# First loads, statistics by pairs, product order and bias product in a graph layer on one core

## The reference

```python
def reference(x, adj, W_self, b_self, W_nb, b_nb, W_comb, b_comb):   # x 8192x256 f32, adj 8192x8192 int32
    h = jnp.maximum(_layernorm(x, axis=-1), 0.0)
    mask = (adj > 0).astype(x.dtype)
    deg = jnp.sum(mask, axis=1, keepdims=True)
    agg = mask @ h / jnp.maximum(deg, 1.0)
    combined = jnp.concatenate([h @ W_self + b_self, agg @ W_nb + b_nb], axis=-1)
    return x + jax.nn.relu(combined @ W_comb + b_comb)
```

## Time and profile before

| what | value |
|---|---|
| median of 3 runs | 1001.75 us (1001.56 to 1003.32) |
| profiled execution, its own time | 1001.76 us |
| its span, first to last instruction | 1000.0 us |
| granted TensorE clock, mean | 1.000 |
| busy PE / DVE / ACT / POOL | 989.9 / 673.9 / 585.0 / 30.5 us |
| DMA | 295 GB/s over the span |
| start of main stage (first L360) | 110.50 us |

### The profile page before, as it was taken

One profiled execution on the slowest core, in us unless ns is written; L12 is line 12 of the kernel. 1 busy time (PEld: TensorE's weight loads), 2 busy tenths in 40 slices (PEclk: granted clock), 3 DMA queues, 4 the chain that ended last, 5 costly groups with the idle time before them and its releaser, 6 DMA issues.

```text
span 1000.0 us, 14269 instructions
## 1 busy us (share of the span) xinstructions
PE 989.9 (99%) x4696; PEld 460.5 (46%) x4696; DVE 673.9 (67%) x1163; ACT 585.0 (59%) x675; POOL 30.5 (3%) x73
## 2 busy tenths in 40 slices
PE   7999999999999999999999999999999999999998
PEld 4555444444444444444444444444444444444443
DVE  6886677986776666766667666676666766667711
ACT  5888886775655556655556555565555655556500
POOL 2332000000000000000000000000000000000000
PEclk9999999999999999999999999999999999999999
DMA  9621399999888898888988888888888888888600
GB/s 344 251 85 43 140 421 371 416 420 377 320 316 321 312 341 317 319 322 312 342 312 322 322 313 336 318 322 322 312 328 328 323 315 321 321 326 326 218 16 10
DMA packets 58994, 295.04 MB, mean 295 GB/s; under 512 B 6624, under 2 KB 24160, under 8 KB 26208
## 3 DMA queue, kind: packets, MB, share of 16 engines
q1 hardware_dynamic: 58976, 294.81, 78.6%
HBM read 286.39 MB, written 8.39 MB: 295 GB/s over the span
## 4 chain that ended last, share of the span: by engine, by line
PE 98%; DMA 1%; DVE 0%; SPq 0%; issue 0%
PE pair_ps L360 89%; PE pair_ps L351 8%; PE turn_ps L333 1%; DMA self_f<-in_x_dram 1%; PE pair_ps L381 0%; DVE x_again L439 0%; SPq L195 0%; SPq L193 0%; DVE z L505 0%; DVE fold L502 0%; DVE x_again L442 0%; DVE part L485 0%; DVE part L482 0%; DVE x_again L488 0%; SPq L177 0%
## 5 line engine op out<-in xcount | busy, mean ns | idle before, releaser
L360 PE MATMUL pair_ps<-z,mask_t 128*128 128x512 f16 x4096 | 885.8, 379 | 0.0
L290 ACT ACTIVATE mask<-mask 128x2048 uint8<-128x2048 uint8 x256 | 488.0, 1908 | 341.4 <-DVE mask_t L430 341.4
L360 PEld LDWEIGHTS pair_ps<-z,mask_t 128*128 128x128 fp8e4 x4096 | 396.2, 98 | 475.7
L430 DVE STREAM_TRANSPOSE mask_t<-mask 128x512 uint32<-128x512 uint32 x256 | 181.7, 710 | 219.8 <-PE pair_ps L360 214.3
L424 DVE TENSOR_SCALAR mask<-stage 128x2048 uint8<-128x2048 int32 x256 | 308.1, 1203 | 6.0 <-DMA stage<-in_adj_dram 5.9
L351 PE MATMUL pair_ps<-mask_t 128*128 128x512 f16 x384 | 87.8, 379 | 0.0
L351 PEld LDWEIGHTS pair_ps<-mask_t 128*128 128x128 f16 x384 | 37.6, 98 | 38.6
L290 ACT ACTIVATION_READ_ACCUMULATOR mask<-mask 128x1 f32 x256 | 48.1, 188 | 0.0
L482 DVE SCALAR_TENSOR_TENSOR part<-pair_ps,rdeg,self_f 128x256 f32<-128x256 f32 x64 | 31.0, 484 | 15.7 <-DVE rdeg L477 11.9
L269 ACT ACTIVATE self_f<-self_f,x_again 128x256 f32<-128x256 f32 x64 | 35.0, 605 | 8.7 <-POOL x_again L260 8.7
L447 DVE SCALAR_TENSOR_TENSOR mask_t<-turn_ps,mask_t 128x512 f16<-128x512 f32 x32 | 21.8, 681 | 19.3 <-ACT mask_t L276 19.3
(11 more groups left out here) (31 smaller groups left out, 93.0 us busy)
## 6 DMA issues: line engine op xcount, KB each, us to landing
stage<-in_adj_dram SPq DMA_DIRECT2D x256, 1024.0 KB, 5.9
self_f<-in_x_dram SPq DMA_DIRECT2D x16, 512.0 KB, 15.4
x_again<-in_x_dram SPq DMA_DIRECT2D x64, 128.0 KB, 5.3
out_dram<-x_again SPq DMA_DIRECT2D x64, 128.0 KB, 5.1
z<-in_L_gnn_W_comb_dram SPq DMA_DIRECT2D x2, 256.0 KB, 4.8
z<-in_L_gnn_W_self_dram SPq DMA_DIRECT2D x1, 256.0 KB, 3.6
z<-in_L_gnn_W_nb_dram SPq DMA_DIRECT2D x1, 256.0 KB, 4.5
z<-in_L_gnn_b_comb_dram SPq DMA_DIRECT2D x1, 128.0 KB, 6.4
```

Of the source, the lines that this page charges most:

```text
L290: act.activation(mask[:, a, :], mask[:, a, :], ACT.Copy, accum_out=deg_part[:, n, a:a + 1]).then_inc(counted, 1)
L360: mm = pe.matmul(acc[n], bytes_of[:, :, s], z16[:, SUB * e + s, :], start=(e == 0 and s == 0), stop=(e == CHUNKS - 1 and s == SUB - 1))
L430: dve.transpose(mask_t[:, n, :, a, :], src).then_inc(transposed, 1)
```

## The change

- **Loads.** The weights are packed by the host into two blocks of 512 KB (4 KB for each partition), one transfer each. The order of issue is weights 0, first half of x chunk 0, weights 1, second half, x chunk 1, the two biases, the rest as before. All from SyncE.
- **Statistics by pairs.** GpSimd works on 128x2 values for each pair. Minus mean moves to VectorE, behind the aggregates. VectorE's `stats_of` runs 4 pairs ahead (before 6).
- **Order.** For pairs 0 to 5 (`CALM = 6`) TensorE runs `project(j)` ahead of `turn(j+2)`; ScalarE and VectorE interleave the weight rounding with the first norms. `project` runs its three terms outermost. Five dummy products of the identity (`WARMING`) stand first on TensorE.
- **Bias product.** VectorE multiplies and adds the four rows of W_comb with the bias column into `part` at steps 8, 9, 10 and 12; a product with ones sums it over partitions behind the last `project`. `c_row` is added there. `fold` moves to step 7.

```diff
+WARMING = 5
+CALM = 6
+BIAS_STEPS = (8, 9, 10, 12)
...
+        ones = x_again[:, 0, 0:P]
+        bc_row = x_again[:, 1, :]
...
-            load_x(0)
-            for n, (dst, w) in enumerate(((ws_t, w_self_t), (wn_t, w_nb_t))):
-                sp.dma_start(dst, w.rearrange("(h p) n -> p h n", p=P)).then_inc(w_loaded[n], DONE)
-                half = slice(n * HALVES, (n + 1) * HALVES)
-                sp.dma_start(wc[:, half, :], w_comb[n * D:(n + 1) * D, :].rearrange("(h p) n -> p h n", p=P)
+            def load_w(n):
+                sp.dma_start(w_all[:, n, :, :].rearrange("p h d -> p (h d)"), weights[n, :, :]
                              ).then_inc(w_loaded[n], DONE)
+            def load_x0(s0, signal):
+                sp.dma_start(self_f[:, s0:s0 + 2, :].rearrange("p s d -> p (s d)"), x[0, :, s0 * D:(s0 + 2) * D]
+                             ).then_inc(signal, DONE)
+            load_w(0)
+            load_x0(0, x_half)
+            load_w(1)
+            load_x0(2, x_full[0])
             load_x(1)
...
-            for e in range(CHUNKS):
-                pool.wait_ge(aggr_done, SUB * (e + 1))
...
+            for p in range(PAIRS):
+                e, s0 = divmod(2 * p, SUB)
+                two = slice(s0, s0 + 2)
+                pool.wait_ge(aggr_done, 2 * (p + 1))
+                pool.tensor_scalar(var_s[:, e % 2, two], mean_var[:, e, two, 1], EPS, H_SCALE ** -2,
                                    ALU.add, ALU.mult).then_inc(var_ready, 1)
+                pool.wait_ge(var_ready, p + 1)
+                pool.tensor_tensor(rstd[:, e, two], var_s[:, e % 2, two], power[:, 0:2], ALU.pow).then_inc(rstd_ready, 1)
+                pool.wait_ge(rstd_ready, p + 1)
+                pool.wait_ge(negated, p + 1)
+                pool.tensor_tensor(shift[:, e, two], minus_mean[:, e % 2, two], rstd[:, e, two], ALU.mult
+                                   ).then_inc(shift_ready, 1)
...
-                act.wait_ge(shift_ready, e + 1)
+                act.wait_ge(shift_ready, j + 1)
...
+            high_of_w(0)
+            norm(0)
+            high_of_w(1)
             high_of_h(0)
+            norm(1)
             norm(2)
...
+                if j == 0:
+                    pe.wait_ge(w_high, 2)
+                    pe.wait_ge(h_high, 1)
+                else:
+                    pe.wait_ge(h_low, j + 1)
+                if j == 1:
                     pe.wait_ge(w_ready, 2)
...
+                for at, (i, w) in enumerate(TERMS):
+                    if j == 0 and w == 1:
+                        pe.wait_ge(w_ready, 2)
+                    if j == 0 and i == 1:
+                        pe.wait_ge(h_low, 1)
+                    for t in range(2):
+                        for half in range(HALVES):
...
+            for _ in range(WARMING):
+                pe.matmul(turn_ps[0][:, 0:P], ident, ident, start=True, stop=True)
...
             for j in range(PAIRS):
+                if j < CALM:
+                    project(j)
                 if j + 2 < PAIRS:
                     turn(j + 2)
-                project(j)
+                if j >= CALM:
+                    project(j)
+            pe.wait_ge(c_part, 2 * HALVES)
+            pe.wait_ge(zeroed, 4)
+            pe.matmul(turn_ps[0][:, 0:D], ones, part[:, :], start=True, stop=True).then_inc(c_product, 1)
...
+                if p >= 4:
+                    dve.wait_ge(shift_ready, p - 3)
+                dve.wait_ge(aggr_done, 2 * (p + 1))
+                dve.tensor_scalar(minus_mean[:, e % 2, s0:s0 + 2], mean_var[:, e, s0:s0 + 2, 0], -1.0, None, ALU.mult
+                                  ).then_inc(negated, 1)
...
+            def sum_of_bias(m):
+                row, col = wc[m // HALVES][:, m % HALVES, :], b_cols[:, m:m + 1]
+                if m == 0:
+                    dve.wait_ge(b_loaded, 2 * DONE)
+                    dve.tensor_scalar(part[:, :], row, col, None, ALU.mult).then_inc(c_part, 1)
+                else:
+                    dve.wait_ge(c_part, m)
+                    dve.scalar_tensor_tensor(part[:, :], row, col, part[:, :], ALU.mult, ALU.add).then_inc(c_part, 1)
+            stats_of(0)
+            stats_of(1)
             w_low(0)
+            stats_of(2)
             w_low(1)
             low_of_h(0)
+            stats_of(3)
...
-                if j + 6 < PAIRS:
-                    stats_of(j + 6)
+                if j + 4 < PAIRS:
+                    stats_of(j + 4)
+                if j in BIAS_STEPS:
+                    sum_of_bias(BIAS_STEPS.index(j))
+                if j == 7:
+                    dve.wait_ge(ident_ready, 1)
...
             dve.wait_ge(fold_ready, QUAD)
+            dve.wait_ge(c_product, 1)
+            dve.tensor_tensor(c_row[:, :], turn_ps[0][:, 0:D], bc_row, ALU.add).then_inc(c_ready, 1)
```

More of the change, by code:

```diff
@@ L42, with graph_layer @@
 RING = 3
+WARMING = 5
+CALM = 6
+BIAS_STEPS = (8, 9, 10, 12)
 MASK_STEPS = (5, 11, 17, 23)
 COUNT_STEPS = (PAIRS - 2, PAIRS - 1, PAIRS, PAIRS)
-def graph_layer(nc, x, adj, w_self_t, w_nb_t, w_comb, b_cols_in, b_comb, out):
-    D = w_comb.shape[1]
+def graph_layer(nc, x, adj, weights, b_cols_in, b_comb, out):
+    D = b_comb.shape[0]
     HALVES = D // P
@@ L96, in early @@
             return late[:, cursor[0] - n:cursor[0]]
[L98 to L103, removed]
+        w_all = early(2 * 2 * HALVES * D).rearrange("p (n h d) -> p n h d", n=2, h=2 * HALVES)
+        w_t = [w_all[:, n, 0:HALVES, :] for n in range(2)]
+        wc = [w_all[:, n, HALVES:2 * HALVES, :] for n in range(2)]
         b_cols = early(2 * HALVES)
+        ones = x_again[:, 0, 0:P]
+        bc_row = x_again[:, 1, :]
         taken = [0]
@@ L128, in graph_layer @@
         b_loaded = sem("b_loaded")
+        x_half = sem("x_half")
         x_full = [sem(f"x_full{e}") for e in range(CHUNKS)]
@@ L291, in count, with high_of_w @@
                                accum_out=deg_part[:, n, a:a + 1]).then_inc(counted, 1)
-            norm(0)
-            norm(1)
-            for n in range(2):
+            def high_of_w(n):
                 act.wait_ge(w_product, n + 1)
@@ L345, in project @@
                     pe.wait_ge(self_copied, j - RING + 1)
[L346 to L352, removed]
+                for at, (i, w) in enumerate(TERMS):
[5 more added lines that the diff above has]
+                        for half in range(HALVES):
+                            mm = pe.matmul(pair_ps[j % RING][:, t, :], h_t[:, j % RING, i, t, half, :], w12[:, w, half, :],
+                                           start=(at == 0 and half == 0),
+                                           stop=(at == len(TERMS) - 1 and half == HALVES - 1))
                 mm.then_inc(projected, 1)
@@ L369, in _ @@
             pe.wait_ge(ident_ready, 1)
-            for n, w_t in enumerate((ws_t, wn_t)):
-                pe.wait_ge(w_loaded[n], 2 * DONE)
+            for _ in range(WARMING):
+                pe.matmul(turn_ps[0][:, 0:P], ident, ident, start=True, stop=True)
+            for n in range(2):
+                pe.wait_ge(w_loaded[n], DONE)
                 for kk in range(HALVES):
                     for m in range(HALVES):
-                        mm = pe.matmul(pair_ps[1][:, n, kk * D:(kk + 1) * D], w_t[:, m, kk * P:(kk + 1) * P],
-                                       wc[:, n * HALVES + m, :], start=(m == 0), stop=(m == HALVES - 1))
+                        mm = pe.matmul(pair_ps[1][:, n, kk * D:(kk + 1) * D], w_t[n][:, m, kk * P:(kk + 1) * P],
+                                       wc[n][:, m, :], start=(m == 0), stop=(m == HALVES - 1))
                 mm.then_inc(w_product, 1)
@@ L401, in tile @@
                     if e == CHUNKS - 4:
+                        if counts:
+                            pe.wait_ge(c_ready, 1)
                         for d in counts:
@@ L434, in stats_of @@
                 if s0 == 0:
-                    dve.wait_ge(x_full[e], DONE)
+                    dve.wait_ge(x_full[e] if e else x_half, DONE)
                     if e >= 2:
                         dve.wait_ge(aggr_done, SUB * (e - 1))
+                if p == 1:
+                    dve.wait_ge(x_full[0], DONE)
                 for s in (s0, s0 + 1):
@@ L518, in _ @@
                     low_of_z(j - 2)
-                if j + 6 < PAIRS:
-                    stats_of(j + 6)
+                if j + 4 < PAIRS:
[4 more added lines that the diff above has]
+                    dve.wait_ge(ident_ready, 1)
+                    for q in range(QUAD):
+                        rows = slice(LANE * q, LANE * (q + 1))
+                        dve.tensor_copy(fold[rows, :], ident[rows, rows]).then_inc(fold_ready, 1)
                 if j in MASK_STEPS:
@@ L561, in _ @@
                 finish(TILES - SUB + n, n)
-_INS = ["x", "adj", "L0_gnn_W_self", "L0_gnn_W_nb", "L0_gnn_W_comb", "biases", "L0_gnn_b_comb"]
+_INS = ["x", "adj", "weights", "biases", "L0_gnn_b_comb"]
 def kernel(**inputs):
@@ L570, with by_partition @@
```

(10 more changed lines are left out.)

17 lines of the change are left out of this document (1 added, 16 removed).

## The result

The changed kernel takes 1005.24 us (median of 7, 1004.56 to 1006.40), the kernel before 1001.75 us (7 runs, 1001.19 to 1003.32). The ratio is 1.0032, 95% interval 1.0021 to 1.0044: slower by 3.5 us. The forecast was 1004.1.

What follows compares the result with a forecast made beforehand. TensorE was taken to bound the kernel, at 98% of the chain that ended last. Terms of -2.3, +0.5 and +4.1 gave +2.3 us on 1001.76, thus 1004.1 us, with a range from 1000.2 to 1008.8.

Steps and rivals of the forecast that it cites:

- Term 1: Start of the kernel: project(0) starts the stream of products at 12.2 instead of turn(2) at 14.49; -2.3 us.
- Term 2: New product with ones in TensorE's stream: two records at 0.25, hidden by nothing; +0.5 us.
- Term 3: Statistics only 4 pairs ahead: a loop over two pairs can't regain lost time, so TensorE waits; +4.1 us.
- neither bound: GpSimd's power on two values: 1.04 us if nothing is saved, 0.20 if it costs like a multiply.
- The loop: Norm, high and low of h, statistics, GpSimd and back over two pairs: 6.15 us against TensorE's 6.05.
- The rival of a whole power: GpSimd's power costs 1.04 us on two values as on four; 1009.2 us, chance 0.20.
- The rival of a clock that stays low until 9.3: TensorE's start: clock low until 9.3 despite the dummies, term 1 only -1.4; 1005.0 us, chance 0.07.
- The rival in which the loop never binds: Statistics loop: norm(9) ends before TensorE is through project(6), no slowdown; 1000.0 to 1000.9 us, chance 0.24.
- The rival in which the weights don't land first: Loads at the start: transfers share the queues, term 1 shrinks toward zero; 1006.4 us, chance 0.02.
- The bias rows: Four bias steps on VectorE, 0.48 us each, covered by idle time but for 0.1 us of term 3.

Runs made afterwards that it cites:

- that part alone in the old kernel: Kernel before with only GpSimd by pairs, minus mean on VectorE and statistics four pairs ahead: 1005.88 us, ratio 1.0037.

## Why the prediction was right, point by point

- **Direction and cause.** Forecast +2.3 us, measured +3.5; range and sign hold. The three terms were off by +0.4, -0.1 and +0.9, so no error hid another. The waits stand where they were forecast, at turns 9, 10, 15, 16, 21, 22, 27 and 28, and they come from the lead of the statistics: shown by one pair more of lead (waits 5.0 to 0.2), by a shorter power with the lead kept (5.0 to 1.0), and by that part alone in the old kernel (0 to 3.5).
- **Term 1, the start: -2.3, measured -1.9.** The first weights landed as forecast, the dummies took 0.23 a record and ended near 4.2. Two inputs were off. The second weights were put at 6.0 and came at 7.9. The 422 GB/s behind that is a row from 12 us; between 4 and 5 us the changed kernel moved 186 GB/s, between 5 and 6 us 301. But the rate is the smaller part: up to 6.5 us the queue had moved the 1.31 MB that reach to the end of the second weights, and when they were there, at 7.91, it had moved 1.87 MB (237 GB/s). The prediction let the transfers land one behind the other, and they didn't. The other input was the delay of 3.3 us between TensorE's first work and the short spacing, from one row. In the runs it was between 3.3 and 6.4 us, with the clock column at 1.00 throughout; in the profile of the changed kernel all of the first eight records kept the long spacing, until 7.7. That the 7 taken for it came near was luck in part: it was a middle between bounds and no result. In this profile the late weights cost TensorE 0.2 us (7.7 to 7.9), and two more slow records 0.4. In the run with chunk 0 as one transfer it was the other way round: short spacing from 5.7, then 1.4 us of standing for the weights, and project(0) at 12.72 against 12.58. What earlier weights and an earlier step would give together was not run.
- **Term 2, +0.5:** measured 0.43, two records at a spacing of 0.216 instead of the 0.25 taken. Its add of c_row was covered.
- **Term 3, +4.1, measured 4.96.** The power was taken at 0.62; measured is 0.69 on two values against 1.04 on four. That is 0.175 us for each value and 0.34 that stays, neither bound but close to the value taken. The loop came to 6.17 us over two pairs (6.15 by the row sums, 6.1 laid out) against 6.05. Minus mean on VectorE takes 0.17 to 0.20, not 0.12. By the starts of the turns, beyond 3.03 us each, TensorE lost 0.8 us at turns 9 and 10 and 1.2, 0.9 and 1.0 behind the other three masks, where 0.8, 1.0, 1.0 and 0.9 were forecast. What was forecast too low lies between them: 0.4 at turns 12 to 14, where the bias rows run and of which leaving three rows out gave 0.2 back, and 0.1 in each two undisturbed pairs (forecast 0.06), as a loop of 6.17 instead of 6.1 makes it. How much of that the power alone brings was not run.
- **The rival of a whole power** (1009.2) fell by the 0.69. The Trainium skill's rate for each element (GPSIMD Engine Reference, section 3.1), with which it went, does not describe a power: two values fewer saved 0.35 us.
- **The rival of a clock that stays low until 9.3** fell in the profile: the second product ran at the short spacing from 7.9. **The rival in which the loop never binds** fell: norm(9) ended at 34.25, while TensorE was through project(6) at 33.8. The lead of five made it true. **The rival in which the weights don't land first** fell for the first block, at 4.14.
- **The bias rows:** forecast 0.1 for four, measured 0.2 for three.

## What to carry to other kernels

When a handover between engines is cut finer, measure the loop that it closes, start to start through every engine's queue, against the time that the bound engine takes for the same number of steps. If it is longer, the bound engine loses a little at every turn and never regains what a disturbance costs, however idle the other engines look. A lead of one step more cost nothing here once the pipeline was full, but the place where the additional step is worked off must itself not stand ahead of something that is waited for. A gain at the start and a loss later are read apart only by the start times of the same instruction in both traces, here the first one of the main stage.

## What the runs showed of the hardware that was not expected

- A mask of VectorE (128x2048, int32 to uint8, 1.2 us) stretches what GpSimd begins 0.15 to 0.17 us behind it: a power from 0.69 to 1.60 us, a multiply from 0.20 to 1.11, in the kernel before L253 from 0.20 to 1.07.
- A scalar_tensor_tensor of VectorE with both inputs in SBUF (128x256 f32, 0.47 us) adds 0.17 us to the power beside it. In all four cases GpSimd's addition is what was left of VectorE's instruction, less about 0.15 us: 1.06, 1.06 and 1.03 us left behind the masks (0.91, 0.91 and 0.87 added), 0.32 behind the row (0.17 added). The Trainium skill (GPSIMD Engine Reference, section 1) names two cases of contention, VectorE in a two-port mode and VectorE with two SBUF inputs. The trace agrees for the second, with 0.17 us; that the mask runs in a two-port mode no row here shows.
- GpSimd's power costs by values: 1.04 us for 128x4, 0.69 for 128x2.
- Transfers of one queue did not land one behind the other. When the second weights were there, 1.87 MB had moved, though 1.31 MB reach to their end (2.09 and 1.57 MB with chunk 0 as one transfer). In the two microseconds from 4 to 6 us the rates were 186 and 301 GB/s in the changed kernel, 336 and 294 in the kernel before, 377 and 344 with chunk 0 as one transfer, and behind 11 us 417 to 422. Why they differ was not settled.
- The records of the weight products (128x256 f32) went from a spacing of 0.43 us to 0.22 us at moments that differ between executions. Behind TensorE's first work it took 3.3 us in the kernel before and 5.9 with the statistics by pairs alone, whose start is the same work, and between 3.3 and 6.4 in the profiles with dummies. The clock column shows 1.00 in all of them.
